# Rows of x split in token order and turned by DMA instead of loaded in squares and turned on VectorE

## What is computed

```python
u = x @ in_proj_w.T + in_proj_b              # 1536 columns
uc = causal 3-tap convolution of each column of u along the tokens + short_b
x0, x1, v = split(uc, 3)
v = fftconv(v * x1, k, filter_bias)          # long convolution, k from a small network
x = layernorm(x + (v * x0) @ out_proj_w.T + out_proj_b)
gate, up = silu(x @ Wg.T), x @ Wu.T          # W = (codes - 128) * scale, 1408 columns
x = layernorm(x + (gate * up) @ Wd.T)
```

## Time and profile before

| what | before |
|---|---|
| median of 3 runs | 990.19 us (988.64 to 991.0) |
| profiled execution | 989.24 us, of which the span of its instructions is 987.4 us |
| TensorE busy | 955.4 us, 97% of the span |
| weight loads busy | 665.8 us, 67% |
| VectorE busy | 762.8 us, 77% |
| ScalarE busy | 437.2 us, 44% |
| GpSimd busy | 555.6 us, 56% |
| chain that ended last, by engine | PE 75%, DVE 9%, issue 5%, POOL 4%, ACT 3% |

### The profile page before, as it was taken

How to read it: one execution, slowest core, us unless ns; L and a number is a source line. 1 busy time by engine, 2 the same in 40 slices (tenths; PEclk the granted TensorE clock), 3 DMA queues, 4 the chain that set the end, 5 groups by cost and what they waited for, 6 DMA issues and landing times.

```text
span 987.4 us, 17405 instructions
## 1 busy us (share of the span) xinstructions
PE 955.4 (97%) x6210; PEld 665.8 (67%) x6210; DVE 762.8 (77%) x1441; ACT 437.2 (44%) x940; POOL 555.6 (56%) x628
## 2 busy tenths in 40 slices
PE   6888999999999999999999999999999999999996
PEld 3345667667676767667676676767677676787774
DVE  6788896887888788787887878787887777686454
ACT  3687543434354343534444343543445344334342
POOL 0268885474747556474765647475564747575210
PEclk9999999999999999999999999999999999999998
DMA  9434400221101211221012211012111110101100
GB/s 300 134 128 131 105 1 1 45 64 22 44 17 27 65 23 43 44 58 27 3 44 44 64 23 44 16 28 65 22 44 23 43 22 10 36 1 44 44 21 22
DMA packets 98953, 47.97 MB, mean 49 GB/s; under 512 B 80048, under 2 KB 84784, under 8 KB 98868
## 3 DMA queue, kind: packets, MB, share of 16 engines
q1 hardware_dynamic: 98370, 46.79, 18.2%
q10 hardware_dynamic: 498, 0.08, 0.0%
HBM read 32.17 MB, written 8.39 MB: 41 GB/s over the span
## 4 chain that ended last, share of the span: by engine, by line
PE 75%; DVE 9%; issue 5%; POOL 4%; ACT 3%; POOLq 0%; DVEq 0%; ACTq 0%
PE gate_up L1316 12%; PE gate_up L1317 12%; PE bank L1159 9%; PE bank L1160 9%; PE bank L1161 9%; PE down L1328 6%; PE down L1329 6%; PE bank L1276 4%; DVE tmp L1068 2%; POOL acc L879 1%; PE spectrum L1159 1%; PE spectrum L1160 1%; PE spectrum L1161 1%; DVE hid_lo L1147 1%; POOL acc L886 1%
## 5 line engine op out<-in xcount | busy, mean ns | idle before, releaser
L885 POOL TENSOR_TENSOR acc<-acc,tmp 128x256 f32<-128x256 f32 x160 | 122.7, 767 | 136.6 <-DVE tmp L1068 124.6
L1068 DVE TENSOR_TENSOR tmp<-spectrum,filt 128x512 f32<-128x512 f32 x256 | 172.7, 681 | 0.5 <-PE spectrum L1161 0.5
L831 ACT ACTIVATE hid<-gate_up,gate_scale 128x256 f32<-128x256 f32 x176 | 82.9, 471 | 195.7 <-PE gate_up L1317 195.6
L1316 PE MATMUL gate_up<-x2T_hi,wg_sb 128*128 128x256 f16 x704 | 163.3, 273 | 0.0
L1317 PE MATMUL gate_up<-x2T_lo,wg_sb 128*128 128x256 f16 x704 | 163.3, 273 | 0.0
L1317 PE MATMUL gate_up<-x2T_lo,wu_sb 128*128 128x256 f16 x704 | 163.3, 273 | 0.0
L1316 PE MATMUL gate_up<-x2T_hi,wu_sb 128*128 128x256 f16 x704 | 163.2, 273 | 0.0
L879 POOL TENSOR_TENSOR acc<-acc,tmp 128x512 f32<-128x512 f32 x96 | 125.3, 1306 | 55.3 <-DVE tmp L1068 55.0
L1159 PE MATMUL bank<-xT_hi,win_hi 128*128 128x512 f16 x360 | 138.1, 384 | 7.2 <-DVE cx L1044 2.3
L838 ACT ACTIVATE hid_hi<-hid 128x256 f16<-128x256 f32 x176 | 73.4, 417 | 145.4 <-DVE hid L1141 145.4
L1160 PE MATMUL bank<-xT_lo,win_hi 128*128 128x512 f16 x360 | 137.8, 383 | 0.0
(11 more groups left out here) (204 smaller groups left out, 1770.8 us busy)
## 6 DMA issues: line engine op xcount, KB each, us to landing
x<-in_x SPq DMA_DIRECT2D x28, 256.0 KB, 2.9
out<-x SPq DMA_DIRECT2D x28, 256.0 KB, 2.1
xstage<-in_x SPq DMA_DIRECT2D x96, 64.0 KB, 2.5
xstage<-in_x SPq DMA_DIRECT2D x12, 256.0 KB, 3.8
more_stages<-in_win SPq DMA_DIRECT2D x7, 256.0 KB, 5.3
x<-in_win SPq DMA_DIRECT2D x5, 256.0 KB, 5.3
acc<-in_decay SPq DMA_DIRECT2D x4, 256.0 KB
x2T_hi<-in_wu SPq DMA_DIRECT2D x4, 256.0 KB, 2.9
```

Source lines behind the costliest of these rows:

```text
L885: G.tensor_tensor(acc[:, i, 0, :], acc[:, i, 0, :], t[:, 1, :], ALU.subtract)
L1068: TT(dst, spectrum[j % 2][:, :, :], k_part, ALU.mult).then_inc(made_done, 1)
L1316: mm(dst, w[:, kb, rows(q)], x2T_hi[:, kb, ts], start=kb == 0, stop=False)
```

## The change

Sequences 1 to 7 (`X_BY_DMA`) are loaded plainly, 4 DMAs of 256 KB each. `xsplit` of these scales and splits the rows as they lie, into a new buffer `x_parts`, in beats 6 to 9 of the odd half, and after each split SP issues two DMA turns, of hi and of lo, into xT_hi and xT_lo. SP waits for the last product that reads the old rows (X0 of block 1 of the odd half) before the first of them; ScalarE no longer does. The first product of the next even half waits for all eight turns. `xturn`, the loads in squares and the TensorE turns of sequence 1 go; with the latter go three entries of `FILLING`, so that `z` of (0, 2) stands ahead of the last split of sequence 1, and the code casts 19 and 20 behind it.

```diff
-BY_SQUARES = range(2, NSEQ)
-SQUARE = 32
+X_BY_DMA = range(1, NSEQ)
...
-    if beat in (9, 10) and n % 2 == 1 and n + 1 < HALVES and (n + 1) // 2 not in BY_SQUARES:
-        steps += [("xt", (n + 1) // 2, 2 * (beat - 9) + b) for b in range(2)]
...
-    if n % 2 == 1 and following in BY_SQUARES:
-        if beat in (2, 3, 4, 5):
-            steps += [("xturn", following, beat - 2)]
-        if beat in (7, 8, 9, 10):
-            steps += [("xsplit", following, beat - 7)]
+    if n % 2 == 1 and following in X_BY_DMA:
+        if beat in (6, 7, 8, 9):
+            steps += [("xsplit", following, beat - 6)]
...
-    ("xt", 1, 1): [("code", 19)],
-    ("xsplit", 1, 0): [("code", 20)],
-    ("xsplit", 1, 1): [("z", 0, 2)],
...
-        turned = sb("turned", [P, L], F32)
+        x_parts = sb("x_parts", [P, TB, 2, D], F16)
...
             def load_x(s, tb):
-                if s - 1 in BY_SQUARES:
-
-                    sp.wait_ge(x_lo_done, TB * by_squares(s - 1) + min(tb + 2, TB))
...
+                if s - 1 in X_BY_DMA:
+
+                    sp.wait_ge(x_lo_done, TB * by_dma_x(s - 1) + tb + 1)
...
-                        sp.dma_start(dst, src).then_inc(x_in[tb], 16)
...
+                row = (s * TB + tb) * P
+                sp.dma_start(xstage[:, tb, :], x[row:row + P, :]).then_inc(x_in[tb], 16)
...
+                elif kind == "xsplit" and at[0] in X_BY_DMA:
+                    s, tb = at
+                    sp.wait_ge(bank_ready, use["ip", 2 * s - 1, 1, X0] + 1)
+                    sp.wait_ge(x_hi_done, TB * s + tb + 1)
+                    sp.dma_start_transpose(xT_hi[:, :, rows(tb)], x_parts[:, tb, 0, :]).then_inc(xt_in, 16)
+                    sp.wait_ge(x_lo_done, TB * by_dma_x(s) + tb + 1)
+                    sp.dma_start_transpose(xT_lo[:, :, rows(tb)], x_parts[:, tb, 1, :]).then_inc(xt_in, 16)
...
-                        act.wait_ge(x_turned, TB * by_squares(s) + tb + 1)
-                        act.wait_ge(bank_ready, use["ip", 2 * s - 1, 1, X0] + 1)
-                        A(xT_hi[:, tb, :], turned_block(tb), ACT.Copy, scale=scale).then_inc(x_hi_done, 1)
+                    if s in X_BY_DMA:
+                        if s > X_BY_DMA[0]:
+                            act.wait_ge(xt_in, 32 * TB * by_dma_x(s))
+                        A(x_parts[:, tb, 0, :], xstage[:, tb, :], ACT.Copy, scale=scale).then_inc(x_hi_done, 1)
...
-                    Vv.transpose(turned_block(kb), xstage[:, kb, :]).then_inc(x_turned, 1)
...
-                        STT(out=xT_lo[:, tb, :], in0=turned_block(tb), scalar=scale, in1=xT_hi[:, tb, :],
+                    if s in X_BY_DMA:
+                        STT(out=x_parts[:, tb, 1, :], in0=xstage[:, tb, :], scalar=scale, in1=x_parts[:, tb, 0, :],
...
-                        if n // 2 in BY_SQUARES:
-                            pe.wait_ge(x_lo_done, TB * by_squares(n // 2) + TB)
+                        if n // 2 in X_BY_DMA:
+                            pe.wait_ge(xt_in, 32 * TB * (by_dma_x(n // 2) + 1))
```

More of the change, by code:

```diff
@@ L180, in beat_steps @@
     following = (n + 1) // 2
-    if n % 2 == 1 and following in BY_SQUARES:
-        if beat in (2, 3, 4, 5):
-            steps += [("xturn", following, beat - 2)]
-        if beat in (7, 8, 9, 10):
-            steps += [("xsplit", following, beat - 7)]
+    if n % 2 == 1 and following in X_BY_DMA:
+        if beat in (6, 7, 8, 9):
+            steps += [("xsplit", following, beat - 6)]
     if n == 3 and beat in (1, 2, 3, 4):
         steps += [("xmax", 2, beat - 1)]
-    if n % 2 == 0 and n // 2 + 1 in BY_SQUARES and n > 2 and beat in (4, 6, 8, 10):
+    if n % 2 == 0 and n // 2 + 1 in X_BY_DMA and n > 2 and beat in (4, 6, 8, 10):
         steps += [("xmax", n // 2 + 1, (beat - 4) // 2)]
@@ L191, in beat_steps @@
         steps += [("x2part", n - 2, 0), ("x2part", n - 2, 1), ("x2dma", n - 2)]
-    if n % 2 == 0 and n // 2 + 1 in BY_SQUARES:
+    if n % 2 == 0 and n // 2 + 1 in X_BY_DMA:
         if n == 2 and beat == 10:
@@ L421, in build @@
         temp_added = sem("temp_added")
-        x_hi_done, x_lo_done, x_turned = sem("x_hi_done"), sem("x_lo_done"), sem("x_turned")
+        x_hi_done, x_lo_done, xt_in = sem("x_hi_done"), sem("x_lo_done"), sem("xt_in")
         tap2_done, tap1_done, v1_done = sem("tap2_done"), sem("tap1_done"), sem("v1_done")
@@ L554, in z_of, with by_dma_x @@
             return zb_hi[:, i % 2, :, :], zb_lo[:, i % 2, :, :]
[L556 to L566, removed]
+        def by_dma_x(s):
+            return min(max(s - X_BY_DMA[0], 0), len(X_BY_DMA))
         def by_dma(m):
@@ L580, in load_x @@
             def load_x(s, tb):
-                if s - 1 in BY_SQUARES:
-                    sp.wait_ge(x_lo_done, TB * by_squares(s - 1) + min(tb + 2, TB))
-                elif s:
-                    sp.wait_ge(bank_ready, use["xt", s - 1, tb] + 1)
+                if s - 1 in X_BY_DMA:
+                    sp.wait_ge(x_lo_done, TB * by_dma_x(s - 1) + tb + 1)
+                elif s == 1:
+                    sp.wait_ge(bank_ready, use["xt", 0, tb] + 1)
                     sp.wait_ge(x_max, TB * (s - 1) + tb + 1)
[L587 to L592, removed]
-                        sp.dma_start(dst, src).then_inc(x_in[tb], 16)
-                else:
-                    row = (s * TB + tb) * P
-                    sp.dma_start(xstage[:, tb, :], x[row:row + P, :]).then_inc(x_in[tb], 16)
+                row = (s * TB + tb) * P
+                sp.dma_start(xstage[:, tb, :], x[row:row + P, :]).then_inc(x_in[tb], 16)
             def load_float(k):
@@ L676, in _ @@
                     if m >= HALVES - 2:
-                        sp.wait_ge(x_lo_done, TB * by_squares(NSEQ))
+                        sp.wait_ge(x_lo_done, TB * by_dma_x(NSEQ))
                         sp.dma_start(xstage[:, tb, :], x[row:row + P, :]).then_inc(x_in[tb], 16)
@@ L752, in _ @@
                     scale = x_scale[:, s % 2:s % 2 + 1]
-                    if s in BY_SQUARES:
-                        act.wait_ge(x_turned, TB * by_squares(s) + tb + 1)
-                        act.wait_ge(bank_ready, use["ip", 2 * s - 1, 1, X0] + 1)
-                        A(xT_hi[:, tb, :], turned_block(tb), ACT.Copy, scale=scale).then_inc(x_hi_done, 1)
+                    if s in X_BY_DMA:
+                        if s > X_BY_DMA[0]:
+                            act.wait_ge(xt_in, 32 * TB * by_dma_x(s))
+                        A(x_parts[:, tb, 0, :], xstage[:, tb, :], ACT.Copy, scale=scale).then_inc(x_hi_done, 1)
                     else:
@@ L896, in _ @@
                     if m >= HALVES - 2:
-                        pool.wait_ge(x_in[tb], 16 * x_blocks(NSEQ) + 16)
+                        pool.wait_ge(x_in[tb], 16 * (NSEQ) + 16)
                     else:
@@ L927, in _ @@
                         dve.wait_ge(ones_set, 3)
-                    dve.wait_ge(x_in[tb], 16 * x_blocks(s + 1))
+                    dve.wait_ge(x_in[tb], 16 * (s + 1))
                     greatest(x_stat[:, s % 2, tb:tb + 1], xstage[:, tb, :]).then_inc(x_max, 1)
@@ L1224, in _ @@
                     dst = free_bank(k)
-                    pe.wait_ge(x_in[tb], 16 * x_blocks(s + 1))
+                    pe.wait_ge(x_in[tb], 16 * (s + 1))
                     if s == 0 and tb == 0:
```

## The result

| what | before | after |
|---|---|---|
| median | 990.30 us (988.64 to 991.0, 4 runs) | 998.61 us (996.83 to 999.78, 4 runs) |
| ratio | | 1.0085, 95% interval 1.0065 to 1.0105 |
| profiled execution; its span | 989.24; 987.4 us | 996.83; 995.0 us |
| VectorE busy | 762.8 us | 752.6 us |
| granted clock, mean | 0.995 | 0.986 |

The kernel is 8.3 us slower. The forecast was 995.0 us with a range to 1001 and 0.73 on slower: the sign held and the time lies in the range; the middle was 3.6 us short.

The account below looks back on a forecast made before the run. TensorE was taken as the bound from 122 to 870 us, with the filling not full. Delay +5.3, clock +1.7 and steady halves -2.2 gave +4.8 us: 995.0 us on the median, range 988.5 to 1001.

Parts of the forecast that it names:

- The first product of half 2 waits for the eighth turn: In the filling, this product waits for eight DMA turns on SP: +5.3 us, bounds 2.3 and 8.3.
- The clock: TensorE's new gap in the filling brings one fall of the granted clock: +1.7 us, bounds 0 and 3.4.
- Nothing is paid back: From the first product of half 2 on, everything moves later with its 5.3 us delay.
- The steady halves: In later halves all five waits for x2T_lo go: -2.2 us, bounds -4.4 and 0.
- part 6: Steady halves: one split leaves the last beat, so x2T_lo waits go, hid_lo waits stay, SP's extra turns are covered: -2.2 us.
- the 4.4 us that are called the most relief can give: From 120 to 880 us, weight loads stand still 2.2 us for the row-turning DMA and 2.2 us for hid_lo.
- the signs that were named: 56 more DMA turns, a long wait before half 2, clock below 1.00, no x2T_lo waits after 290 us, later stretch 2 us shorter.
- VectorE's 16.8 us less work: VectorE loses 24 turns of 0.70 us; beside a full TensorE this counts for nothing but the steady waits.
- Late in every sequence: Rival: SP starts steady turns over 5.3 us late; 1 us over costs six sequences 6 us: 1001.0 us, chance 0.06.
- paid back: Rival: TensorE's idle at 90 to 122 us absorbs 2.1 us, clock doesn't fall: +1.0, 991.2 us, chance 0.14.
- faster: Rival: splits bind the eight turns, 2.1 us paid back, all 4.4 us of steady waits gone: -4.2, 986.0 us, chance 0.13.
- short issues: Rival: turns issue as fast as plain loads, the last right behind its split: +3.4, 993.6 us, chance 0.05.

Follow-up runs that it names:

- experiment 5: Changed kernel plus 18 matmuls on constants ahead of the wait for sequence 1's turns: 994.73 us; the same 18 over 8 columns instead of 512: 996.35 us.
- experiments 3 and 9: 3: changed kernel, sequence 1's four splits moved earlier, 997.13 us. 9: sequence 1 back on TensorE, later sequences' splits at beats 6, 6, 9, 9, 990.28 us.
- the small matmuls: Changed kernel plus 18 matmuls over 8 columns instead of 512, ahead of the wait for sequence 1's turns: 996.35 us.
- experiment 7: Changed kernel with one DMA turn of 128 x 1024 for both halves of a block instead of two of 128 x 512, every sequence: 997.34 us.
- experiment 1: Changed kernel with sequence 1 put back on TensorE in the old filling order, sequences 2 to 7 on DMA turns: 989.38 us, ratio 0.9995.

## Why the prediction was right or wrong

**The first product of half 2 waits for the eighth turn: right, 1 us short.** Forecast +5.3, measured +6.27. SP's 1.25 us per turn, the two code loads between, z ahead of the last split and the 1 us of idle there came as worked out. Counted from the last product that reads the old rows, the fifth turn was due 8.64 us later and started 9.61 later, and from there all went as forecast. Of this 1 us, 0.4 came with the first split (0.75 taken from rows of which none took over 0.753, 1.16 measured; six more splits of the kernel before, which read the tile `turned` and stand in no row, took 0.73 to 1.30); 0.3 lay between the second split's end at 85.12 and its turn's start at 85.46, which no run explains; and 0.2 was the second code load (0.33 taken, 0.57 measured beside the turns). The third and fourth splits were slow too (1.43 and 1.07), but their turns stood in SP's queue, and they cost nothing.

**The clock: right.** Forecast +1.7, measured +1.64 in the trace of the change and 1.76 between the two of experiment 5. The price was read from the fall at 62 to 66 us, where TensorE waits 2.04 us. Of the twelve traces with that wait of 2.03 to 2.04 us only three show the clock below 1.00 in the 4 us behind it (before, and experiments 3 and 9), so it was chance that the trace of before had such a fall to read. That the larger gap would bring a fall was a guess, and it held: ahead of the first product of half 2 the clock was at 0.50 in all four traces in which TensorE stood idle for it for over 5 us (the change twice, the small matmuls, experiment 7).

**Nothing is paid back: right.** The shift of +6.5 at 98 us stays between 6.1 and 7.0.

**The steady halves: wrong.** Forecast -2.2 with bounds -4.4 and 0, measured +0.4, outside them. The step that failed is the one of part 6 (and of the 4.4 us that are called the most relief can give): it took the idle time of the weight loads as TensorE's. The waits of the matmuls from 122 to 870 us in the kernel before were 1.4 us, none of them for the turns. That all five waits of the weight loads would go was right, and worth nothing that shows. The waits for hid_lo, which the forecast kept, grew from 0.3 to 0.8 us. Of the signs that were named, the one on this stretch (about 2 us shorter) failed; the others came. VectorE's 16.8 us less work were counted at nothing, rightly; its busy time fell by 10.2 us only, the 28 splits taking 0.95 us each on average where the 18 from xstage before took 0.75.

**Not foreseen:** the reload at the end, +0.7 us, and the spread of the executions. Of the thirteen traces the five with a packet of instruction load beside the reload had it land in 4.1 to 4.7 us, and TensorE then waited 0.4 to 1.0 us for hid_lo; the other eight had it land in 2.8 to 3.0, without that wait. The sum for the profiled executions is +6.27 + 1.64 - 1.37 + 0.4 + 0.7 = 7.6 us, their difference. The medians differ by 0.7 more, since the profiled execution after was the fastest of its four. So the forecast's 4.8 us were 1 short in the filling and 2.6 short in the steady halves; the 1.37 us by which this execution was ahead earlier in the filling hides part of that, and it is chance.

**The rivals.** "Late in every sequence" fell with experiment 1, "paid back" and "faster" with the timeline, "short issues" with SP's rows: 1.20 to 1.29 us each, so the eighth turn went out 1.09 us after the last split's end and not right behind it.

## What to carry to other kernels

In a pipeline's filling, ask what stands between the data and the first use, not which engine is relieved: an operation moved off a busy engine onto an in-order queue still costs its full latency there, and whatever shares that queue (here the code loads) is late in its place. Bound what a full engine can win by the waits of its own work, here of the matmuls, not by those of the loads that run ahead of it. Price an instruction by a row that has the same neighbours and the same operands' places, and keep the clock in the sum where a gap grows, as here to 5.81 us.

## What the runs showed that was not expected

- A DMA turn holds SP about as long for 128 x 1024 values (1.23 us) as for 128 x 512 (1.19 to 1.26).
- One VectorE split with both operands in SBUF takes 0.68 us alone and 1.27 beside GpSimd, and GpSimd's instructions grow as well.
- The same wait of TensorE of 2.04 us in the filling was followed by a granted clock of 0.59 and 0.56 in the trace before and of 1.00 in the trace after. The product behind it ended 1.7 us later in the one, in work that the change leaves alone: a difference between two single executions that no edit made.
- With eighteen matmuls of next to no work more, ahead of a wait that hides them, no packet of instruction load lay beside the last reload, and the median was 2.1 us lower. A packet beside this transfer of 256 KB was seen with 1.1 to 1.9 us on its landing. That the instruction count moves the packets, and that they delay the landing, is not shown.
